# Modulated conv chain folded to one five-tap filter per sample: third and fourth sample of each group by shared products of even and odd columns

## The reference

```python
s = style @ mw.T + mb
weight = SCALE * w * s[:, None, :, None]
demod = lax.rsqrt(jnp.sum(weight * weight, axis=(2, 3)) + EPS)
weight = weight * demod[:, :, None, None]
# 'same':       conv of 3 taps, padded by 1
# 'upsample':   transposed conv of stride 2, then blur [1,3,3,1]/4
# 'same':       conv of 3 taps, padded by 1
# 'downsample': blur [1,3,3,1]/8, then conv of 3 taps, stride 2
```

## Time and profile before

| | |
|---|---|
| median of 3 runs | 757.55 us (754.91 to 758.24) |
| the profiled execution's own time | 756.94 us |
| its span, first to last instruction | 755.1 us |
| mean granted TensorE clock | 0.982 |
| PE busy | 711.5 us (94%) |
| PEld busy | 622.0 us (82%) |
| DVE busy | 342.5 us (45%) |
| ACT busy | 299.5 us (40%) |
| POOL busy | 281.6 us (37%) |
| DMA | 108.46 MB, mean 144 GB/s, 58.6% of 16 engines in SP's queue |

### The profile page before, as it was taken

The page is one execution under the profiler, slowest core; times in us unless marked ns, Lnnn a source line. Parts: engine busy times, 40 slices in busy tenths (PEclk is TensorE's granted clock), DMA queues, the critical chain, the costliest instruction groups (busy, mean ns, idle before and its releaser), DMA issues.

```text
span 755.1 us, 10500 instructions
## 1 busy us (share of the span) xinstructions
PE 711.5 (94%) x3858; PEld 622.0 (82%) x3858; DVE 342.5 (45%) x551; ACT 299.5 (40%) x437; POOL 281.6 (37%) x456
## 2 busy tenths in 40 slices
PE   5668999998999999998999999999899999999997
PEld 4557888887888888887888888888788888888886
DVE  5968434435544333445335443453454443334430
ACT  3322444343434344434243444443334444443432
POOL 2431443442333443333443434434334434443310
PEclk9979999999999999999999999999999999999999
DMA  7043267764367767655756666677445777666572
GB/s 253 1 118 64 84 147 175 175 147 118 99 162 175 157 145 166 154 138 115 175 120 155 151 152 148 150 175 175 107 108 137 174 175 170 148 150 164 157 177 83
DMA packets 112162, 108.46 MB, mean 144 GB/s; under 512 B 4528, under 2 KB 78640, under 8 KB 112112
## 3 DMA queue, kind: packets, MB, share of 16 engines
q1 hardware_dynamic: 111456, 106.22, 58.6%
q10 hardware_dynamic: 656, 1.57, 0.6%
HBM read 36.47 MB, written 33.55 MB: 93 GB/s over the span
## 4 chain that ended last, share of the span: by engine, by line
PE 77%; DVE 10%; issue 6%; POOL 3%; ACT 2%; DMA 1%; POOLq 0%; ACTq 0%; DVEq 0%
PE po L159 16%; PE po L161 16%; PE po L160 16%; PE pg L159 7%; PE pg L161 6%; PE pg L160 6%; PE pg L164 3%; PE pg L165 3%; POOL Q2l L520 2%; DVE xl L595 1%; DVE Wf L617 1%; DVE Q2f L606 1%; POOL Q2h L168 1%; ACT Q2h L418 1%; ACT W L428 1%
## 5 line engine op out<-in xcount | busy, mean ns | idle before, releaser
L159 PE MATMUL po<-xh,W 128*128 128x512 f32 x640 | 254.5, 398 | 0.0
L160 PE MATMUL po<-xl,W 128*128 128x512 f32 x640 | 253.4, 396 | 0.0
L161 PE MATMUL po<-xh,W 128*128 128x512 f32 x640 | 253.4, 396 | 0.0
L595 DVE TENSOR_TENSOR xl<-X,xh 128x1032 fp32r<-128x1032 f32 x64 | 81.8, 1277 | 201.3 <-ACT xh L396 201.1
L403 ACT ACTIVATE T<-po,cv,DD 128x512 f32<-128x512 f32 x128 | 99.7, 779 | 169.2 <-PE po L161 167.7
L161 PEld LDWEIGHTS po<-xh,W 128*128 128x128 f32 x640 | 125.2, 196 | 24.5
L159 PEld LDWEIGHTS po<-xh,W 128*128 128x128 f32 x640 | 125.8, 197 | 20.6 <-issue 0.2
L160 PEld LDWEIGHTS po<-xl,W 128*128 128x128 f32 x640 | 125.6, 196 | 20.1
L520 POOL TENSOR_TENSOR Q2l<-Q2f,Q2h 128x512 fp32r<-128x512 f32 x31 | 40.0, 1290 | 228.3 <-ACT Q2h L418 228.3
L428 ACT CAST W<-Wf 128x512 fp32r<-128x512 f32 x64 | 46.6, 728 | 119.3 <-DVE Wf L617 93.0
L613 DVE TENSOR_TENSOR Gf<-pg,D10c 128x512 f32<-128x512 f32 x64 | 44.0, 689 | 103.8 <-PE pg L165 103.6
(11 more groups left out here) (154 smaller groups left out, 998.2 us busy)
## 6 DMA issues: line engine op xcount, KB each, us to landing
X<-in_xin SPq DMA_DIRECT2D x64, 516.0 KB, 5.3
out<-T SPq DMA_DIRECT2D x64, 512.0 KB, 3.1
W<-W SPq DMA_DIRECT2D x96, 256.0 KB, 6.6
W<-W SPq DMA_DIRECT2D x32, 384.0 KB, 7.6
E<-in_ed ACTq DMA_DIRECT2D x1, 768.0 KB, 8.5
XE<-in_xe SPq DMA_DIRECT2D x1, 576.0 KB, 11.1
Gf<-in_mwt SPq DMA_DIRECT2D x1, 256.0 KB, 3.2
A2f<-in_a ACTq DMA_DIRECT2D x1, 256.0 KB, 6.3
```

The costliest lines, as they stand in the source:

```text
L159: eng.matmul(o, wh_, rh, start=first, stop=False)
L160: eng.matmul(o, wh_, rl, start=False, stop=False)
L161: return eng.matmul(o, wl_, rh, start=False, stop=last)
L595: tt(xl[:, n % XH], X[:, n % XR], r32(xh[:, n % XH]), ALU.subtract).then_inc(s_xl, 1)
```

## The change

The conv of samples i = 2 and 3 of each group (the odd pairs) is computed differently; i = 0 and 1 stay. The 512 output columns of an odd pair's sample are kept as 256 even and 256 odd columns. With e and o the even and odd columns of x, the host lays an odd pair out as [e | o], each HW = 258 wide, POOL forms a third part and replaces the first one, [e - o | o | e' - o] with e' shifted by one (`x_parts`), and the five taps become three short products: m with taps W0+W1, W2+W3, W4 on o, shared by both halves of the output; taps 0, 2, 4 on e - o for the even columns; taps 1, 3 on e' - o for the odd columns. That is 8 taps of 256 columns x 3 matmuls = 24 matmuls of 256 columns instead of 15 of 512. The sums of taps are formed on DVE (`sums`), split by ACT (`sums_high`) and DVE (`sums_low`) and copied across partitions by three more DMAs on SP's queue (`cross_sums`). The shared product goes from its own PSUM bank `pm` through ACT (`m_out`, 256 columns) into `M`, and the output of an odd pair is written by DVE, `po` times demodulation plus `M`, instead of by ACT. `X` gets 3 buffers instead of 4, `xh` and `xl` 2 instead of 3; a row is 774 wide, of which an even pair uses 516 and an odd pair 774. `x_high` and `x_low` run one pair ahead instead of two, and `x_low` moves behind `full` and `w_low` in its slot. The edge steps of chunks 1 to 3 move from slot 3 to slot 2.

```diff
-XR = 4
-XH = 3
+HW = L2 // 2 + 2
+XW = 3 * HW
+XR = 3
+XH = 2
...
-                edge_at[(EC // NG * c - 5 + k, 3)] = (c, k)
+                edge_at[(EC // NG * c - 5 + k, 2)] = (c, k)
...
+            def cross_sums(g):
+                w, v = r32(W[:, g % 2]), r32(V[:, g % 2])
+                sp.wait_ge(s_vh, 2 * g + 2)
+                sp.wait_ge(s_vl, 2 * g + 2)
+                sp.dma_start(v[hi, :, :, 1], v[lo, :, :, 0]).then_inc(s_v[g % 2], 16)
+                sp.dma_start(v[lo, 0, :, 1], w[hi, 0, :, 1, 0]).then_inc(s_v[g % 2], 16)
+                sp.dma_start(v[lo, 1, :, 1], r32(Vx[hi])).then_inc(s_v[g % 2], 16)
...
                 if g + 1 < NGR:
                     cross(g + 1, 0)
                     cross(g + 1, 1)
+                    cross_sums(g + 1)
                 store(n)
...
+                if n % 2 == 0:
+                    if g:
+                        pe.wait_ge(s_tf, 2 * g - 1 + q)
+                    part(po[b % 2][:, :], (0, 1, 2, 3, 4), 0).then_inc(s_o, 1)
+                    return
+                k = b // NG * 2 + q
+                if q == 0:
+                    pe.wait_ge(s_v[g % 2], 16 * 3 * (g // 2 + 1))
+                pe.wait_ge(s_vl, 2 * g + 2)
+                if k:
+                    pe.wait_ge(s_m, k)
+                part(pm[:, 0:256], (5, 6, 4), HW).then_inc(s_mm, 1)
+                pe.wait_ge(s_td, 2 * g + 1 + q)
+                part(po[b % 2][:, 0:256], (0, 2, 4), 0)
+                part(po[b % 2][:, 256:512], (1, 3), 2 * HW).then_inc(s_o, 1)
...
+            def m_out(b):
+                k = b // NG * 2 + b % Q
+                act.wait_ge(s_mm, k + 1)
+                if k >= 2:
+                    act.wait_ge(s_tf, k - 1)
+                act.activation(M[:, k % 2, :], pm[:, 0:256], ACT.Identity,
+                               bias=cv[:, b:b + 1], scale=DD[:, 3, b:b + 1]).then_inc(s_m, 1)
+
+            def sums_high(g):
+                act.wait_ge(s_vf, g + 1)
...
+                act.copy(V[:, g % 2, :, 0, 0], Vf[:, 0:3:2]).then_inc(s_vh, 1)
...
+                act.copy(Vx[:, 0], Vf[:, 1]).then_inc(s_vh, 1)
...
-                if b:
+                if b and b % NG in (1, 2):
                     t_out(b - 1)
-                if b % Q == 0 and b // Q + 2 < NQ:
-                    x_high(b // Q + 2)
+                if b % Q == 0 and b // Q + 1 < NQ:
+                    x_high(b // Q + 1)
                 for x in units_of(b):
                     if x[1] != 5:
                         high(*x)
+                    if x[1] == 6:
+                        sums_high(x[0])
+                if i >= 2:
+                    m_out(b)
...
+            def x_parts(n):
+                pool.wait_ge(s_x[n % XR], 16 * (n // XR + 1))
+                x = X[:, n % XR]
+                pool.tensor_tensor(x[:, :, 2 * HW:3 * HW], x[:, :, 1:HW + 1], x[:, :, HW:2 * HW], ALU.subtract
+                                   ).then_inc(s_ab, 1)
+                pool.wait_ge(s_ab, n)
+                pool.tensor_tensor(x[:, :, 0:HW], x[:, :, 0:HW], x[:, :, HW:2 * HW], ALU.subtract).then_inc(s_ab, 1)
...
                 if i == 0 and g + 1 < NGR:
                     identity(g + 1)
+                if i == 1 and g + 1 < NGR:
+                    x_parts(b // Q + 3)
                 for x in units_of(b):
                     if x[1] < 4:
                         low(*x)
...
+            def sums(g):
+                dve.wait_ge(s_ce, cnt(g, 5))
+                if g:
+                    dve.wait_ge(s_vh, 2 * g)
+                tt(Vf[:], Wf[:, 1, 0:3], Wf[:, 1, 1:4], ALU.add).then_inc(s_vf, 1)
+
+            def sums_low(g):
+                dve.wait_ge(s_vh, 2 * g + 1)
+                tt(V[:, g % 2, :, 1, 0], Vf[:, 0:3:2], r32(V[:, g % 2, :, 0, 0]), ALU.subtract).then_inc(s_vl, 1)
+                dve.wait_ge(s_vh, 2 * g + 2)
+                tt(Vx[hi, 1], Vf[hi, 1], r32(Vx[hi, 0]), ALU.subtract).then_inc(s_vl, 1)
...
-                if b % Q == 0 and b // Q + 2 < NQ:
-                    x_low(b // Q + 2)
+                if i in (3, 0) and b:
+                    t_out(b - 1)
                 for x in units_of(b):
                     full(*x)
-                if (x := units_of(b)) and x[0][1] == 4:
-                    w_low(x[0][0], 0)
-                    w_low(x[0][0], 1)
+                    if x[1] == 5:
+                        sums(x[0])
+                    if x[1] == 6:
+                        w_low(x[0], 0)
+                        w_low(x[0], 1)
+                        sums_low(x[0])
+                if b % Q == 0 and b // Q + 1 < NQ:
+                    x_low(b // Q + 1)
...
+            t_out(B - 1)
```

More of the change, by code:

```diff
@@ L54, in build @@
         xl = sb("xl", [128, XH, Q, XW], F32R)
+        M = sb("M", [128, 2, 256])
         T = sb("T", [128, TR, Q, L2])
@@ L58, in build @@
         W = sb("W", [128, 2, 5, 2, 2, 2, 128], F32R)
+        Vf = sb("Vf", [128, 3, 128])
+        V = sb("V", [128, 2, 2, 2, 2, 128], F32R)
+        Vx = sb("Vx", [128, 2, 128], F32R)
         Gf = sb("Gf", [128, 2, 4, 128])
@@ L127, in build @@
         pe_ = psum("pe")
-        ps = psum("ps")
+        pm = psum("pm")
+        ps = pm
         s_in = {n: sem("i_" + n) for n in ("mwt", "st", "bb", "wt", "q3", "a2", "cw", "b1", "ed", "xe", "eye")}
@@ L220, in _ @@
             cross(0, 1)
+            cross_sums(0)
             for g in range(NGR):
@@ L248, in conv, with part @@
                     pe.wait_ge(s_xl, n + 1)
[L249 to L255, removed]
+                def part(o, blocks, x):
+                    for j, v in enumerate(blocks):
+                        w = [(W[:, g % 2, v, t, i // 2] if v < 5 else V[:, g % 2, v - 5, t]
+                              ).rearrange("p r (o b) -> p (r o) b", b=2)[:, :, i % 2] for t in range(2)]
+                        m = split_mm(pe, o, w[0], w[1], *[t[:, n % XH, q, x + j:x + j + o.shape[1]] for t in (xh, xl)],
+                                     j == 0, j == len(blocks) - 1)
+                    return m
+                if n % 2 == 0:
[13 more added lines that the diff above has]
+                part(po[b % 2][:, 256:512], (1, 3), 2 * HW).then_inc(s_o, 1)
             def unit(g, u):
@@ L392, in x_high @@
             def x_high(n):
-                act.wait_ge(s_x[n % XR], 16 * (n // XR + 1))
+                if n % 2:
+                    act.wait_ge(s_ab, n + 1)
+                else:
+                    act.wait_ge(s_x[n % XR], 16 * (n // XR + 1))
                 if n >= XH:
                     act.wait_ge(s_o, Q * (n - XH + 1))
-                act.copy(xh[:, n % XH], X[:, n % XR]).then_inc(s_xh, 1)
+                w = XW if n % 2 else 2 * HW
+                act.copy(xh[:, n % XH, :, 0:w], X[:, n % XR, :, 0:w]).then_inc(s_xh, 1)
+            def m_out(b):
[7 more added lines that the diff above has]
+                act.wait_ge(s_vf, g + 1)
+                if g >= 2:
+                    act.wait_ge(s_o, NG * (g - 1))
+                act.copy(V[:, g % 2, :, 0, 0], Vf[:, 0:3:2]).then_inc(s_vh, 1)
+                if g:
+                    act.wait_ge(s_v[(g - 1) % 2], 16 * 3 * ((g - 1) // 2 + 1))
+                act.copy(Vx[:, 0], Vf[:, 1]).then_inc(s_vh, 1)
             def t_out(b):
@@ L471, in _ @@
             high(0, 6)
-            x_high(1)
+            sums_high(0)
             q3_high(2)
@@ L542, in finish @@
             def finish(n):
-                pool.wait_ge(s_t, Q * (n + 1))
+                pool.wait_ge(s_tf if n % 2 else s_td, Q * (n // 2 + 1))
                 pool.wait_ge(s_ed, 5 * (n * Q // EC) + 5)
                 e = T[:, n % TR, :, :]
-                pool.tensor_copy(e[:, :, 0:2], EP[:, n * Q:(n + 1) * Q, 0:2])
-                pool.tensor_copy(e[:, :, L2 - 2:L2], EP[:, n * Q:(n + 1) * Q, 2:4]).then_inc(s_fin, 1)
+                a, z, d = (0, 255, 256) if n % 2 else (0, L2 - 2, 1)
+                pool.tensor_copy(e[:, :, a:a + d + 1:d], EP[:, n * Q:(n + 1) * Q, 0:2])
+                pool.tensor_copy(e[:, :, z:z + d + 1:d], EP[:, n * Q:(n + 1) * Q, 2:4]).then_inc(s_fin, 1)
             pool.wait_ge(s_k0, K_B1)
@@ L560, in _ @@
             low(1, 1)
+            x_parts(1)
             q3_full(2)
@@ L594, in x_low, with t_out @@
                 dve.wait_ge(s_xh, n + 1)
-                tt(xl[:, n % XH], X[:, n % XR], r32(xh[:, n % XH]), ALU.subtract).then_inc(s_xl, 1)
+                w = XW if n % 2 else 2 * HW
+                tt(xl[:, n % XH, :, 0:w], X[:, n % XR, :, 0:w], r32(xh[:, n % XH, :, 0:w]), ALU.subtract).then_inc(s_xl, 1)
+            def t_out(b):
+                n, q = divmod(b, Q)
+                k = b // NG * 2 + q
+                dve.wait_ge(s_m, k + 1)
+                dve.wait_ge(s_o, b + 1)
+                if q == 0 and n >= TR:
+                    dve.wait_ge(s_st[n % TR], 16 * (n // TR))
+                dve.scalar_tensor_tensor(out=T[:, n % TR, q].rearrange("p (e k) -> p e k", e=2),
```

(15 more changed lines are left out.)

12 lines of the change are left out of this document (6 added, 6 removed).

## The result

The changed kernel takes 829.0 us (median of 4 runs, 822.4 to 837.3) against 757.15: a ratio of 1.092, 95% interval 1.081 to 1.104. Ratios and intervals leave out executions in a slower state, here the one of 837.3 us; it stands in the median and in the range. The profiled execution took 834.5 us and spans 832.5.

The account below looks back on a forecast made before the run. PE bounds with nothing to spare, so delays in the DVE-ACT-POOL chain feeding unit 2 idle it. On 756.9 us: 29 groups x (23.9 - 20.95) = +86, edges +9, prologue +1, end -2.5: 850 us, range 765 to 870.

Parts of the forecast that it names:

- the ring: Closed chain of waits setting a group's length, through DVE, ACT and POOL to PE's unit 2: 22.3 us forecast before clock loss.
- rival 1: Same chain, but idle shorter or placed so the clock stays up: 804 us, chance 0.2.
- PE's gain: Odd pair's sample on PE falls from 3.51 to 2.87 us, 0.64 less, 41 us over 64 samples.
- Rival 4: Strided weights make PE's 256-column matmuls cost more than 0.1195 us; at 0.15 around 880 us; chance 0.05 including worse.
- DVE in slot 0: DVE's sums and `x_low` delay Q2f from +7.3 to +8.7; PE idles 1.6 us, group 21.1 us.
- The load and `x_parts`: In POOL's slot 1, late load and `x_parts` delay `low` to +11.4; PE idles 2.9 us, group 22.3 us.
- the lock: A DVE operation with both inputs in SBUF holds POOL off; `x_parts` waits for `x_low`, until +8.7.
- The clock: PE's 2.9 us idle in each group lowers its clock, costing 1.6 us more in each: 23.9 us.
- Edges: Edge steps moved to slot 2: DVE chain delays unit 3's `full`; +3 us a chunk, +9 in all.
- End: The last two groups have no units and gain their 2 x 1.3 = 2.5 us.
- rival 3: DVE's slot-0 work and `x_parts` both fit, PE bounds again: 726 us, chance 0.12.
- Rival 2: POOL's `x_parts` is out of the way, only DVE's 1.4 us delay is left: 768 us, chance 0.12.

Follow-up runs that it names:

- e5: Changed kernel with `x_parts` at the end of POOL's slot 1, W copies early, odd pair's `x_low` later, behind a wait for POOL's subtractions: 739.0 us.
- e4: Changed kernel with edges back in slot 3, `x_parts` at the end of POOL's slot 1 and W copies ahead of the store: 793.6 us.
- e8: As e5 but without DVE's wait for POOL's subtractions before the odd pair's `x_low`: 766.0 us.
- e3: Changed kernel with the four copies of W issued on SP ahead of the store: 834.8 us.
- e1: Changed kernel with the edge steps of chunks 1 to 3 put back in slot 3: 846.8 us.
- e6: As e5, with edge steps split: PE's matmuls in slot 2, DVE's chain in slot 3 behind `t_out` and `full`: 727.7 us.
- e9: e3 with 18 matmuls on constants, whose results nothing reads, ahead of unit 2's wait: 806.5 us.
- e12: e6 with `x_parts` back at the head of POOL's slot 1: 784.6 us.

## Why the prediction was right

The forecast was 850 us, in a range of 765 to 870, and the direction, the ring and its members came out. The 829.0 lies in the middle between the forecast and rival 1 (the same chain with the clock up, 804), and the groups were of both kinds. Of the signs that I named, a mean clock of 0.93 (0.935), the first `x_parts` held until `x_low` ended and Q2f right behind `x_low` are there. Not there are 2.9 us of idle before unit 2 in each steady group, a fall behind each, and groups of 23.9 us; PE's busy time went down by 1.6 us only.

- **PE's gain**: 0.1195 us a matmul forecast, 2.90/24 = 0.121 measured, with strided weights too. The sample's 0.64 us were 0.61. Rival 4 is out.
- **DVE in slot 0**: Q2f forecast at +8.7 behind a 1.9 us `x_low`; the trace has it at +8.9, at the end of a 1.77 us `x_low`. e5, which moves `x_low` and holds POOL's order, takes 1.5 us off e4's group. Shown.
- **The load and `x_parts`**: landing 4.6 us after issue (forecast 4.5), during `x_low`; the lock as forecast, 2.59 against 1.10 us, and shown again in e8. The two operations took 1.10 each and not 1.29, 0.4 us less in all; the group without falls was 22.1 and not 22.3. The Trainium skill ("SBUF — State Buffer", section "SBUF: two separate sides") has the loser fully blocked until the other is done; the 2.59 agrees.
- **The clock** is the term that was mis-sized. A fall costs 1.45 us a group (23.55 against 22.1 in e3), near the 1.6 taken, but I let it fall in each of the 29 groups (+46 us) and it fell in seven of the 15 undisturbed ones. Those took 341 us, not 15 x 23.9 = 358. Two steps stand behind it. One is the sentence "The conv's waits for `M`, `V` and `po` are met a slot or more ahead", which leaves out the conv's wait for W. In four of the eight groups without a fall the copies of W land late at the conv and split the idle, as in the 1.3 and 0.9 us above; in e3, where it is never split, the clock fell in 11 of 15. Each is the count of one execution. The other is the step from one stall of 2.73 us to "An idle of 2.9 in each group should cost 1.6 more in each": in the other four groups the idle was one piece, of 2.0 to 2.9 us, and the clock stayed up, and why stays open.
- **How near it came is in part luck.** In the profiled execution, 834.5 us and so 15.5 below the forecast, the undisturbed groups added 19 us less than forecast (25.5 against 15 x 2.95 = 44) and the edges 2.5 less, but the start and the end some 6 more. The median of the runs is another 5.5 us below the profiled one.
- **Edges**: a chunk was forecast at 4 x 23.9 + 13.2 = 108.8 us and took 107.9. That is right in the sum; how it divides between clock and chain I can't say, and that slot 2 made it dearer is refuted by e1.
- **End**: forecast -2.5, measured some +4, with a fall in the last groups. The start took +5.7 in the group behind the first, forecast +4 (its share of the 29 groups, and +1 for the prologue).
- **Rivals**: rival 3 (PE bounds again, 726 us) named as its point Q2f by +7.3 and `low` by +8.7. e6 reaches both and takes 728. Rival 2 (only DVE's 1.4 us left) is e4 in kind: groups of 21.3 us for the 21.05 of its sum, though e4's edges put its whole at 794 and not 768. Rival 1 is what eight of the changed kernel's 15 undisturbed groups did, and e9 comes near it as a whole (806.5 us for 804).

## What to carry to other kernels

When a change relieves the bounding engine of a kernel that has no slack, list for every other engine what now stands in its queue ahead of the chain that feeds the bound: here two operations on POOL, 1.2 us of sums (0.95 forecast) and a 1.8 us subtraction on DVE, and copies behind a store took back the 41 us forecast as PE's gain and 72 more. The same arithmetic in another order, with one wait more, was worth 100 us (829 to 728). Test such places together: moving the copies of W alone gave nothing that can be told from the scatter (835 against 829), and it was worth 96 us once the rest was right.

## What was not expected of the hardware

Whether the clock falls is not settled by the length of one idle: it fell behind 1.81 us in the changed kernel, 1.95 us in e12 and 2.38 us in e3, and stayed up behind 2.92 us in the changed kernel. But 1.64 us in each undisturbed group of e4 and 1.16 to 1.33 us in each of e8 brought no fall in any of them. In between, the same program scatters: runs of the changed kernel lie 1.5% apart (822.4 to 834.5) where e5's and e8's lie 0.2% apart. Why one idle of such a length brings a fall and another doesn't stays open. Filling 2 us of idle with matmuls that do nothing made a kernel 28 us faster.
